# Two transformer layers on one core: setup ordered with the rest, query lengths as scale of the exponential, padded streams

## The chip, the cores and the metric

One NeuronCore of a Trainium2 chip runs the whole program. The time is that of the device, in microseconds; lower is better. The engines have short names: PE is TensorE, ACT ScalarE, DVE VectorE, POOL GpSimd, and SP the queue that issues the DMAs.

## The reference, cut to what matters

The input is 16 sequences of 256 tokens with 128 channels. First a mixing step is computed and added to each sequence, between two modulated layer norms. Then two layers follow, each with windowed attention (8 heads of 64, a query sees its own and the preceding 64 tokens' window) and a gated feed-forward (hidden size 341).

```python
h = shift_token(x)                      # upper 64 channels come from the token before
q, k, v = split(h @ wqkv)               # 3 x 512
q = l2norm(q) * qs;  k = l2norm(k) * ksc
q, k = rotary_xpos(q, k)
o = local_attention(q, k, v)            # softmax over q . k * 8, masked
x = x + o @ wo
h = shift_token(x)
h = (h - mu) / sqrt(var + 1e-5) * lg + lb
a, g = split(h @ w1 + b1)
x = x + (a * gelu(g)) @ w2 + b2
```

The outer part is an adaLN block: shift, scale and gate come from silu(c) @ wmod, per sequence; the output is the input, the gated mixing step and the gated feed-forward part together.

## The kernel before

The work comes in eight half-units of two sequences (512 tokens, four tiles of 128). A "turn" has four slots; slots 0 and 1 do layer 1's projections and layer 0's feed-forward of the two half-units of one unit, slots 2 and 3 layer 0's projections and layer 1's feed-forward, and attention runs one slot behind the projections it needs. So there are 16 attention passes of four tiles, 16 feed-forwards and 16 projection blocks of four tiles, in a pipeline over six lists of steps.

What runs in which order is written out by hand for each engine: `ORDER["pe"]`, `ORDER["act"]`, `ORDER["dve"]` and `ORDER["pool"]` each hold six lists, and `every_turn` issues their steps in that order. The engines meet only through semaphores, so a step waits in its engine's queue for what it needs, and all behind it wait too. SP has no list: it issues loads and stores slot by slot (lines 632 to 661 and `turn`).

Streams are held transposed (channels on partitions, tokens along the free axis), in `y_new` and `y_t`. Matrix products with w_qkv and w1 are taken in three parts: both operands are split into a rounded high part and a low part (`h_hi`, `h_lo`, `wq_hi`, `wq_lo`, `w1_hi`, `w1_lo`).

- *Setup* (lines 699 to 717 on PE, 935 on ACT, 1131 to 1188 on DVE, 1431 to 1448 on POOL) runs ahead of the lists, except two parts of DVE's (`finish_setup`), which follow two steps of the first list. It turns the parameter rows into columns, makes modulation and gates, the guides' unit lengths (by Newton steps on DVE), the rotary tables, and the high and low parts of the weights.
- *Projections*: "split" shifts the stream into `shifted` by two ACT copies (983, 984), DVE rounds it (1380), POOL takes the low part (1483). Per tile and q or k, ACT squares (1083) and for q copies (1087), DVE multiplies by the rotary tables (1391, 1393) and sums the squares per head (1398), POOL multiplies the cosine part of q (1491) and adds (1494) into `qk`. ACT copies v (1093) and the half tile that the next tile's window reads into `v_cross` (1092).
- *Unit lengths*: per pair of tiles DVE bounds the sums (1404), POOL raises 32 columns to the power -0.5 (1454), and DVE multiplies q and k of both tiles by the root (1195).
- *Attention*, per tile: "turn" transposes q and k (PE 696, ACT 950 and 954), "score" puts mask and products into PSUM (746, 759), DVE takes the negated maximum (1215), ACT four exponentials for each of two halves (964), "flip" transposes them (696, 972), "mix" multiplies by v (785), DVE divides (1223, 1227), "out" transposes (978), and "project" after four tiles multiplies by w_o (727); DVE adds it to the stream (1207).
- *Feed-forward*: the shift again (983, 984), transposes, statistics and norm (1235 to 1244), transposes back, an ACT evacuation with gain and bias (997), DVE rounding (1265), POOL's low part (1470), three chunks up with Gelu (795 to 797, 1012, 1273), down (831), sum (1280).

The few lines on which the attention's edit turns:

```python
act.activation(probs[:, ring, hh, :], banks[m][:, hh * P:(hh + 1) * P], ACT.Exp,
               bias=neg_max[:, ring, hh:hh + 1], scale=1.0)
...
return pool.tensor_tensor(to, of, minus_half[:, 0:of.shape[-1]], ALU.pow)
```

## Time and profile before

| | |
|---|---|
| median of three runs | 967.34 us (966.5 to 968.35) |
| the profiled execution | 966.96 us, its span 965.0 us |
| mean granted TensorE clock | 0.942 of full |
| busy: PE, DVE, ACT, POOL | 786.4, 668.0, 659.3, 539.6 us |

Busy time of PE is modelled from pipelined matmuls. An arrow in a row names what ended the idle time before an instruction. The chain is followed back from the last instruction to what released each step; "issue" in it is time for which the profile shows nothing that was waited for. L1207 is line 1207 of the kernel.

### The profile page before, as it was taken

How to read it: one execution, taken by the hardware profiler on the slowest of the kernel's cores; microseconds unless marked ns; L12 is line 12 of the kernel's file. 1: busy time of each engine (PE TensorE's matmuls, PEld its weight loads, DVE VectorE, ACT ScalarE, POOL GpSimd, SP SyncE). 2: the span in 40 equal slices, each digit the busy share in tenths (PEclk: the TensorE clock that was granted, in tenths of full speed). 3: DMA queues.
4: the chain of work that ended last, by engine and by line, in shares of the span. 5: the costliest groups of instructions: out<-in, count | busy, mean ns of one | idle time of the engine just before them, and what ended most of it. 6: DMA issues, size and time to landing. Idle time of an engine off the chain costs nothing.

```text
span 965.0 us, 19306 instructions
## 1 busy us (share of the span) xinstructions
PE 786.4 (81%) x7151; PEld 556.3 (58%) x7151; DVE 668.0 (69%) x1588; ACT 659.3 (68%) x1545; POOL 539.6 (56%) x324
## 2 busy tenths in 40 slices
PE   4456788879889989888969979888888989888874
PEld 4334566656556666655657656656565666656543
DVE  4566876685687877586887967486787776676732
ACT  0234766867576985877786886877675887868672
POOL 2046853493956653394985643293966690576600
PEclk9668789999899999999999999999999999999997
DMA  6000000000000000000000000000000000000000
GB/s 206 0 12 1 12 2 1 1 1 2 1 2 1 23 2 22 2 1 1 1 1 2 23 1 23 1 2 1 1 1 2 12 2 13 2 1 2 1 1 22
DMA packets 12275, 9.85 MB, mean 10 GB/s; under 512 B 1040, under 2 KB 11288, under 8 KB 12184
## 3 DMA queue, kind: packets, MB, share of 16 engines
q1 hardware_dynamic: 12184, 8.64, 3.0%
q8 instruction: 57, 0.93, 0.4%
q14 instruction: 34, 0.28, 0.1%
HBM read 6.54 MB, written 2.10 MB: 9 GB/s over the span
## 4 chain that ended last, share of the span: by engine, by line
PE 40%; DVE 20%; ACT 19%; issue 11%; POOL 9%; DMA 0%; SPq 0%; POOLq 0%; ACTq 0%; DVEq 0%
ACT probs L964 7%; PE pair L696 6%; PE mixed L727 5%; POOL qk L1494 4%; PE dense L831 4%; PE pair L759 3%; DVE space L1393 3%; DVE q_norm L1398 3%; PE dense L795 3%; PE dense L796 2%; PE dense L797 2%; DVE qk L1195 2%; PE dense L908 2%; ACT squares L1083 2%; ACT probs_t L972 2%
## 5 line engine op out<-in xcount | busy, mean ns | idle before, releaser
L1494 POOL TENSOR_TENSOR qk<-space 128x512 f32<-128x512 f32 x128 | 186.4, 1463 | 58.0 <-DVE q_norm L1398 55.1
L1454 POOL TENSOR_TENSOR root<-power,minus_half 128x32 f32<-128x32 f32 x32 | 174.0, 5438 | 4.6 <-DVE power L1404 4.6
L964 ACT ACTIVATE probs<-pair,neg_max 128x128 f32<-128x128 f32 x512 | 138.3, 402 | 18.9 <-DVE neg_max L1215 18.5
L1393 DVE TENSOR_TENSOR space<-dense,tables 128x512 f32<-128x512 f32 x128 | 87.5, 684 | 36.9 <-ACT space L1087 35.2
L908 PE MATMUL dense<-wq_hi,h_hi 128*128 128x512 f32 x192 | 90.2, 470 | 26.6 <-DVE space L1393 10.9
L1491 POOL TENSOR_TENSOR space<-space,tables 128x512 f32<-128x512 f32 x64 | 82.7, 1293 | 50.7 <-ACT space L1087 50.7
L696 PE MATMUL pair<-eye_s,probs 128*128 128x128 f32 x512 | 80.9, 292 | 34.9 <-ACT probs L964 34.7
L1215 DVE TENSOR_REDUCE neg_max<-pair 128x4 f32<-128x512 f32 x128 | 82.0, 684 | 35.2 <-PE pair L759 35.1
L1083 ACT ACTIVATE squares<-dense 128x512 f32<-128x512 f32 x128 | 79.1, 618 | 39.5 <-PE dense L910 38.6
L696 PEld LDWEIGHTS pair<-eye_s,probs 128*128 128x128 f32 x512 | 59.1, 146 | 56.2 <-ACT probs L964 51.9
L1398 DVE TENSOR_REDUCE q_norm<-squares 128x8 f32<-128x512 f32 x128 | 86.4, 675 | 0.0
L1195 DVE TENSOR_TENSOR qk<-qk,root 128x2048 f32<-128x2048 f32 x32 | 81.1, 2534 | 1.7 <-POOL root L1454 1.7
L909 PE MATMUL dense<-wq_lo,h_hi 128*128 128x512 f32 x192 | 78.4, 409 | 0.0
L910 PE MATMUL dense<-wq_hi,h_lo 128*128 128x512 f32 x192 | 78.3, 408 | 0.0
L1483 POOL TENSOR_TENSOR h_lo<-shifted,h_hi 128x512 fp32r<-128x512 f32 x16 | 20.3, 1268 | 103.3 <-DVE h_hi L1380 103.3
L972 ACT ACTIVATE probs_t<-pair 128x512 f32<-128x512 f32 x128 | 72.5, 645 | 4.4 <-PE pair L696 3.6
L1273 DVE SCALAR_TENSOR_TENSOR space<-dense,columns,space 128x512 f32<-128x512 f32 (+1 forms) x48 | 35.9, 749 | 56.3 <-ACT space L1012 45.7
L759 PEld LDWEIGHTS pair<-k_t,q_t 64*64 64x64 f32 x2048 | 55.2, 133 | 27.1 <-issue 27.1
L759 PE MATMUL pair<-k_t,q_t 64*64 64x128 f32 (+1 forms) x2048 | 70.7, 263 | 0.0
L696 PE MATMUL pair<-eye_s,qk 128*128 128x128 f32 x512 | 65.4, 275 | 5.3 <-issue 2.8
L696 PEld LDWEIGHTS pair<-eye_s,qk 128*128 128x128 f32 x512 | 57.1, 141 | 18.6 <-issue 10.7
L727 PE MATMUL mixed<-o_t,wo_s 128*128 128x512 f32 x128 | 62.4, 634 | 5.4 <-ACT o_t L978 5.4
(166 smaller groups left out, 1809.2 us busy)
## 6 DMA issues: line engine op xcount, KB each, us to landing
x_in<-n_L_attn_embeddings_dram SPq DMA_DIRECT2D x8, 256.0 KB, 3.0
out_dram<-hn SPq DMA_DIRECT2D x8, 256.0 KB, 2.4
qk<-in_L_ffn_wqkv_dram SPq DMA_DIRECT2D x1, 1536.0 KB, 6.2
qk<-in_L_ffn_w_dram SPq DMA_DIRECT2D x1, 682.0 KB, 7.5
wo_s<-in_L_ffn_wo_dram SPq DMA_DIRECT2D x2, 256.0 KB
o_t<-in_L_wmod_dram SPq DMA_DIRECT2D x1, 384.0 KB, 3.3
probs<-const_rotary_dram SPq DMA_DIRECT2D x1, 256.0 KB, 3.6
band_s<-const_band_dram SPq DMA_DIRECT2D x1, 256.0 KB, 7.8
```

The source lines that it names most:

```text
L696: last = pe.transpose(to[:, k * P:(k + 1) * P], rows(k), eye_s[:, :])
L727: last = pe.matmul(mixed[:, :], wo_s[:, layer, k, :], o_t[:, k, :], start=(k == 0), stop=(k == 3))
L759: last = pe.matmul(banks[m][w * WIN:(w + 1) * WIN, hh * P:hh * P + n], q_t[rows, t % 2, hh, w * WIN:(w + 1) * WIN], keys, start=False, sto ...
L908: pe.matmul(to[:, :], h_hi[:, rows], wq_hi[:, layer, cols], start=True, stop=False)
L964: last = act.activation(probs[:, ring, hh, :], banks[m][:, hh * P:(hh + 1) * P], ACT.Exp, bias=neg_max[:, ring, hh:hh + 1], scale=1.0)
L972: act.activation(probs_t[:, 2 * (t % 2) + m, :, :], banks[m][:, :].rearrange("p (k n) -> p k n", k=4), ACT.Copy).then_inc(flip_kept, 1)
L1083: last = act.activation(squares[:, m, :], src[:, :], ACT.Square)
L1195: dve.tensor_tensor(rows, rows, root[:, :].rearrange("p (h o) -> p h o", o=1) .broadcast_to([P, 4 * HEADS, DH]), ALU.mult).then_inc(qk_rea ...
L1393: dve.tensor_tensor(turned_s[:, t % 2, m, :].rearrange("p (h a b) -> p h a b", h=HEADS, a=2), halves[:, :, ::-1, :], rot(layer, t, 2 * m + 1),
L1398: dve.tensor_reduce(q_norm[:, 16 * (t % 2) + 8 * m:16 * (t % 2) + 8 * m + 8], squares[:, m, :].rearrange("p (h d) -> p h d", h=HEADS), AX_ ...
L1454: return pool.tensor_tensor(to, of, minus_half[:, 0:of.shape[-1]], ALU.pow)
L1494: pool.tensor_tensor(qk[s][:, t, m * INNER:(m + 1) * INNER], turned_c[:, t % 2, m, :], turned_s[:, t % 2, m, :], ALU.add).then_inc(added, 1)
```

## The change

All four order lists are written anew, with finer steps: turn, flip and mix are each split in two halves (the second number of `3:a.flip.0.1`), feed-forward "up" on PE in gate and value part, and the projections' work on DVE and POOL in "tile", "norm", "cos", "add", "root" and "unit". Gelu's three steps follow each other on ACT with only copies between. Setup becomes steps in the first list, each with its own semaphore: the roundings of w_qkv are on ACT, the guides' root is a power on POOL, and a step "bias" folds the feed-forward norm's gain and bias into w1 and b1.

The streams get a column of zeros in front of each sequence (`SEQ + 1`), and every shift is read in place: the rounding is two DVE copies of 64 partitions each, the low part is half on POOL and half on DVE, and the feed-forward's first transposes are eight matmuls against halves of the identity. `v_cross` is written by DMAs from `v`, on SP's queue, between loads and stores. The inverse root is by a seed (DVE) and three Newton steps (POOL), per stream and pair of tiles; the query's root is the scale of the exponentials, and the maximum is multiplied by it; keys are multiplied tile by tile.

```diff
-        y_new = [sb(f"y_new{s}", [P, 2, SEQ]) for s in range(2)]
-        y_t = [sb(f"y_t{s}", [P, 2, SEQ]) for s in range(2)]
+        y_new = [sb(f"y_new{s}", [P, 2, SEQ + 1]) for s in range(2)]
+        y_t = [sb(f"y_t{s}", [P, 2, SEQ + 1]) for s in range(2)]
...
+            def cross_values(i, slot, p):
+                s = stream(slot)
+                if runs(i, slot, (PROJ,), turns):
+                    for t, half_ in ((2 * p, 1), (2 * p + 1, 0)):
+                        sp.wait_ge(*read_at(i, slot, (PROJ, "tile", t, 2)))
+                        rows = slice(WIN * half_, WIN * half_ + WIN)
+                        sp.dma_start(v_cross[s][rows, p, :, :], v[s][rows, t, :, :]).then_inc(v_crossed[s][p], 16)
+            for i in range(turns + 1):
+                for slot in range(4):
+                    cross_values(i, slot, 0)
+                    if slot > 1:
+                        s = stream(slot)
+                        if runs(i, slot, (STORE,), turns):
+                            store_result(i, slot)
+                        if i < turns - 1:
+                            sp.wait_ge(x_used[s], i + 1)
+                            load_x(i + 1, s)
+                    cross_values(i, slot, 1)
...
-                    pe.wait_ge(qk_ready, 2 * before + t // 2 + 1)
+                    if m == 0:
+                        pe.wait_ge(added, 2 * tau + 1)
+                    else:
+                        pe.wait_ge(keys_ready, tau + 1)
...
-                    done(turn_four(to, lambda k: flat(shifted)[:, k * P:(k + 1) * P]),
-                         i, slot, step)
+                    for k in range(TILES):
+                        at = (k % 2) * P
+                        for part in range(2):
+                            last = pe.matmul(to[:, k * P + part * WIN:k * P + (part + 1) * WIN],
+                                             y_t[stream(slot)][:, k // 2, at + 1 - part:at + 1 - part + P],
+                                             eye_s[:, part * WIN:(part + 1) * WIN], start=True, stop=True)
+                    done(last, i, slot, step)
...
-                                                  bias=neg_max[:, ring, hh:hh + 1], scale=1.0)
+                                              bias=neg_max[:, ring, hh:hh + 1],
+                                              scale=query_root(s, t, m)[:, hh:hh + 1])
...
-                    act.activation(hn[:, :], src[:, :], ACT.Identity, scale=columns[:, ROW_LN_G + layer:ROW_LN_G + layer + 1],
-                                   bias=columns[:, ROW_LN_B + layer:ROW_LN_B + layer + 1]).then_inc(empty(i, slot, step), 1)
+                    wait_split_free(act, i, slot, FF)
+                    act.wait_ge(*filled_at(i, slot, step))
+                    act.activation(h_hi[:, :], bank(i, slot, step)[:, :], ACT.Copy).then_inc(ff_hi, 1)
...
-                        act.activation(v_cross[s][half_rows, t // 2, :, 0:DH], heads[half_rows], ACT.Copy)
...
+                                      ALU.max, negate=True).then_inc(max_self, 1)
+                    dve.wait_ge(max_self, 2 * tau + m + 1)
+                    dve.wait_ge(qk_rooted, 2 * before + t // 2 + 1)
+                    dve.tensor_tensor(neg_max[:, ring, :], neg_max[:, ring, :], query_root(s, t, m),
+                                      ALU.mult).then_inc(maxed, 1)
...
+                elif what == "lo":
+                    dve.wait_ge(ff_hi, before + 1)
+                    src = bank(i, slot, (FF, "norm"))
+                    dve.tensor_tensor(h_lo[:, :], src[:, :], h_hi[:, :].bitcast(F32),
+                                      ALU.subtract).then_inc(empty(i, slot, (FF, "norm")), 1)
...
+                    keys = qk[s][:, t, INNER:].rearrange("p (h d) -> p h d", d=DH)
+                    dve.tensor_tensor(keys, keys, key_root(s, t).rearrange("p (h o) -> p h o", o=1)
+                                      .broadcast_to([P, HEADS, DH]), ALU.mult).then_inc(keys_ready, 1)
...
+            def unit_root(to, pair_):
+                y, z = to[:, 0, :], to[:, 1, :]
+                count = NEWTON * pair_ + 1
+                pool.wait_ge(qk_seeded, pair_ + 1)
+                pool.tensor_tensor(z, y, half[:, :], ALU.mult).then_inc(qk_newton, 1)
+                pool.wait_ge(qk_newton, count)
+                for k in range(3):
+                    pool.tensor_tensor(scratch[:, :], y, z, ALU.mult).then_inc(qk_newton, 1)
+                    pool.wait_ge(qk_newton, count + 1)
+                    pool.tensor_tensor(scratch[:, :], threes[:, :], scratch[:, :], ALU.subtract).then_inc(qk_newton, 1)
+                    pool.wait_ge(qk_newton, count + 2)
+                    if k < 2:
+                        pool.tensor_tensor(to[:, :, :], to[:, :, :], scratch[:, :].rearrange("p (o h) -> p o h", o=1)
+                                           .broadcast_to([P, 2, 32]), ALU.mult).then_inc(qk_newton, 1)
+                        count = count + 3
+                        pool.wait_ge(qk_newton, count)
+                    else:
+                        pool.tensor_tensor(y, y, scratch[:, :], ALU.mult).then_inc(qk_rooted, 1)
...
-                        pool.wait_ge(summed, 2 * tau + m + 1)
+                        if before >= 2:
+                            pool.wait_ge(turned, 8 * (before - 2) + 2 * t + m + 1)
+                        pool.wait_ge(*read_at(i, slot, (PROJ, "tile", t, m)))
```

## Rows read from the trace of the kernel before

**Rows 1.** The page, part 1: busy us, share of the span, instructions, by engine.
```profile
PE 786.4 (81%) x7151; PEld 556.3 (58%) x7151; DVE 668.0 (69%) x1588; ACT 659.3 (68%) x1545; POOL 539.6 (56%) x324
```

**Rows 2.** The page, part 4: the chain that ended last, by engine.
```profile
PE 40%; DVE 20%; ACT 19%; issue 11%; POOL 9%; DMA 0%; SPq 0%; POOLq 0%; ACTq 0%; DVEq 0%
```

**Rows 3.** Windows: busy us (instructions) per engine, granted clock, DMA share, GB/s.
```profile
0.00:61.00 61.00, 25.22 (x95) 20.34 (x95) 31.17 (x113) 9.88 (x27) 11.02 (x26) 0.75 0.28 86
61.00:151.40 90.40, 69.83 (x550) 50.06 (x550) 66.69 (x164) 53.88 (x143) 56.79 (x37) 0.83 0.01 4
151.40:939.10 787.70, 679.15 (x6472) 478.21 (x6471) 561.88 (x1290) 587.61 (x1364) 469.52 (x261) 0.98 0.02 5
939.10:965.00 25.90, 12.19 (x40) 7.69 (x38) 8.27 (x22) 7.97 (x12) 2.27 (x2) 0.74 0.07 20
```

**Rows 4.** Line 1207, the residual sum after attention: durations, first and last start.
```profile
L1207 DVE TENSOR_TENSOR y_t<-y_new,mixed x8: 674/684/689, 151.4 to 848.8; 128x512 f32<-128x512 f32 x8
L1207 DVE TENSOR_TENSOR y_t<-y_t,mixed x8: 671/686/690, 260.0 to 939.1; 128x512 f32<-128x512 f32 x8
```

**Rows 5.** Waits of PE from 150 to 900 us: total, times, longest.
```profile
PE pair L696 <- ACT probs L964: 23.8, 44, 2.3
PE mixed L785 <- ACT probs_t L972: 12.4, 16, 2.1
PE pair L746 <- ACT k_t L954: 11.0, 16, 1.5
```

**Rows 6.** Instruction groups of ACT: count, busy us, mean ns, idle time before.
```profile
L983 ACT ACTIVATE shifted<-y_t 64x512 f32<-64x512 f32 x24 | 15.1, 628 | 28.2 <-DVE y_t L1207 22.7 <-DVE y_t L1280 5.5
...
L1092 ACT ACTIVATE v_cross<-dense 64x512 f32<-64x512 f32 x64 | 38.2, 596 | 8.4 <-PE dense L910 6.2
...
L964 ACT ACTIVATE probs<-pair,neg_max 128x128 f32<-128x128 f32 x512 | 138.3, 402 | 18.9 <-DVE neg_max L1215 18.5
...
L1030 ACT ACTIVATE y_new<-dense,mod 128x256 f32<-128x256 f32 x16 | 8.2, 572 | 20.0 <-PE dense L696 20.0
...
L1108 ACT ACTIVATE hn<-y_t,mod 128x256 f32<-128x256 f32 x16 | 7.3, 508 | 7.2 <-DVE y_t L1280 7.2
```

**Rows 7.** Instruction groups of DVE.
```profile
L1195 DVE TENSOR_TENSOR qk<-qk,root 128x2048 f32<-128x2048 f32 x32 | 81.1, 2534 | 1.7 <-POOL root L1454 1.7
...
L1380 DVE CAST h_hi<-shifted 128x512 fp32r<-128x512 f32 x16 | 7.7, 483 | 8.0 <-ACT shifted L984 8.0
```

**Rows 8.** Small DVE products: line 1315's group, then line 1317's min, median, max.
```profile
L1315 DVE TENSOR_TENSOR col<-col,root_n 128x4 f32<-128x4 f32 x8 | 3.2, 402 | 1.4 <-POOL root_n L1454 1.4
...
L1317 DVE TENSOR_TENSOR col<-col x8: 161/163/1143, 33.9 to 708.8; 128x4 f32<-128x4 f32 x8
```

**Rows 9.** Instruction groups of POOL.
```profile
L1494 POOL TENSOR_TENSOR qk<-space 128x512 f32<-128x512 f32 x128 | 186.4, 1463 | 58.0 <-DVE q_norm L1398 55.1
...
L1454 POOL TENSOR_TENSOR root<-power,minus_half 128x32 f32<-128x32 f32 x32 | 174.0, 5438 | 4.6 <-DVE power L1404 4.6
...
L1470 POOL TENSOR_TENSOR h_lo<-hn,h_hi 128x512 fp32r<-128x512 f32 x16 | 23.7, 1484 | 61.0 <-DVE h_hi L1265 61.0
...
L1444 POOL TENSOR_TENSOR tables<-probs 128x128 f32<-128x128 f32 x8 | 3.3, 450 | 0.0
```

**Rows 10.** The chain in order of time: start us, us, what.
```profile
190.91 5.29 issue
...
771.77 5.23 issue
```

**Rows 11.** The page, part 6, DMA issues: KB each, us to landing.
```profile
x_in<-n_L_attn_embeddings_dram SPq DMA_DIRECT2D x8, 256.0 KB, 3.0
```

**Rows 12.** Timeline, start and tail: start us, us, engine, line, idle before.
```profile
28.89 3.36 DVE L1182 TENSOR_TENSOR wq_lo<-qk,wq_hi 128x3072 fp32r<-128x3072 f32 x1
...
939.84 0.63 ACT L983 ACTIVATE shifted<-y_t 64x512 f32<-64x512 f32 x1 [2.46 <-DVE y_t L1207]
...
949.82 0.79 PE L795 MATMUL dense<-h_hi,w_hi 128*128 128x512 f32 x1 [2.74 <-POOL h_lo L1470]
```

More of the change, by code:

```diff
@@ new lines @@
+        2:a.mix.3.1 3:a.turn.0.0 2:proj.tile.1.2 2:proj.tile.2.0 2:a.out.3 2:proj.tile.2.1 2:a.project
+        2:proj.tile.2.2 2:proj.tile.3.0 2:proj.tile.3.1 2:proj.tile.3.2 3:a.turn.0.1 3:a.turn.1.0
+        3:a.turn.1.1 2:ff.norm 3:a.score.0 2:new.mix 3:a.score.1 2:new.sum 2:ff.up.0.0 2:ff.up.0.1
+        2:ff.up.1.0 2:ff.up.1.1 2:ff.up.2.0 2:ff.up.2.1 2:ff.down 2:new.stream 3:a.flip.0.0 3:a.flip.0.1
+        2:store.turn 3:ff.stats 3:a.mix.0.0 3:a.mix.0.1 3:a.flip.1.0 3:proj.tile.0.0 3:a.flip.1.1
@@ new lines @@
+        2:proj.tile.1.1 2:a.mix.2.0 2:a.mix.2.1 2:a.flip.3.0 2:a.flip.3.1 2:a.out.2 2:a.mix.3.0 2:a.mix.3.1
+        3:a.turn.0.0 2:proj.tile.1.2 2:a.out.3 2:proj.tile.2.0 2:a.project 2:proj.tile.2.1 2:proj.tile.2.2
+        2:proj.tile.3.0 2:proj.tile.3.1 2:proj.tile.3.2 3:a.turn.0.1 3:a.turn.1.0 2:ff.norm 3:a.turn.1.1
+        3:a.score.0 2:new.mix 3:a.score.1 2:new.sum 2:ff.up.0.0 2:ff.up.0.1 2:ff.up.1.0 2:ff.up.1.1
+        2:ff.up.2.0 2:ff.up.2.1 2:ff.down 2:new.stream 3:a.flip.0.0 3:a.flip.0.1 2:store.turn 3:ff.stats
@@ L145 @@
+        2:a.flip.2.0 2:a.flip.2.1 2:a.mix.2.0 2:a.flip.3.0 2:a.mix.2.1 2:a.flip.3.1 2:a.out.2 2:a.mix.3.0
+        2:a.mix.3.1 2:store.turn 2:a.out.3 2:a.project 3:ff.stats 3:ff.norm 3:ff.up.0.0 3:ff.up.0.1
+        3:ff.up.1.0 3:ff.up.1.1 3:ff.up.2.0 3:ff.up.2.1 3:ff.down 3:store.turn"""),
     ],
@@ L281 @@
-        2:new.stream 2:ff.up.0 2:ff.up.1 2:ff.up.2 3:a.unit 2:ff.down 3:proj.split 3:a.score.0 3:a.score.1
-        2:store.turn 2:proj.keep 3:proj.tile.0.0 3:proj.tile.0.1 3:a.mix.0 3:proj.tile.1.0 3:new.stats
-        3:proj.tile.1.1 3:new.turn 3:proj.rsqrt.0 3:proj.tile.2.0 3:proj.tile.2.1 3:a.mix.1 3:ff.stats
-        3:a.score.2 3:ff.norm 3:a.score.3 3:proj.unit.0 3:new.dots 3:a.mix.2 3:proj.tile.3.0 3:new.sims
-        3:a.mix.3 3:new.weights 3:ff.hi 3:proj.tile.3.1 3:new.gate 3:new.again 3:ff.up.0 3:proj.rsqrt.1
@@ L297 @@
-        2:new.weights 2:proj.tile.0.1 2:proj.tile.1.0 2:proj.tile.1.1 2:proj.rsqrt.0 2:proj.tile.2.0
-        2:proj.tile.2.1 2:ff.stats 2:a.score.2 2:a.score.3 2:proj.unit.0 2:ff.norm 2:a.mix.2 2:proj.tile.3.0
-        2:a.mix.3 2:proj.tile.3.1 2:new.gate 2:ff.hi 2:new.again 2:a.project 2:proj.rsqrt.1 2:new.stream
-        2:ff.up.0 2:ff.up.1 2:ff.up.2 3:a.unit 2:ff.down 3:proj.split 3:a.score.0 3:a.score.1 2:store.turn
-        2:proj.keep 3:proj.tile.0.0 3:proj.tile.0.1 3:a.mix.0 3:proj.tile.1.0 3:proj.tile.1.1 3:proj.rsqrt.0
@@ new lines @@
+        2:proj.tile.3.0 2:proj.tile.3.1 2:proj.norm.3.0 2:proj.norm.3.1 2:proj.root.1 2:ff.lo 3:a.score.0.0
+        2:new.gate 2:proj.unit.2 2:proj.unit.3 2:ff.up.0 2:ff.up.1 2:new.again 2:ff.up.2 3:a.score.0.1
+        2:new.stream 2:ff.down 3:a.score.1.0 3:a.score.1.1 2:store.turn 3:proj.hi 2:proj.keep 3:proj.lo
+        3:ff.stats 3:a.mix.0.0 3:a.mix.0.1 3:ff.norm 3:a.mix.1.0 3:proj.tile.0.0 3:a.mix.1.1 3:proj.norm.0.0
+        3:proj.norm.0.1 3:proj.tile.0.1 3:new.stats 3:a.score.2.0 3:a.score.2.1 3:proj.norm.1.0
@@ new lines @@
+        2:proj.tile.3.0 2:proj.tile.3.1 2:proj.norm.3.0 2:proj.norm.3.1 2:proj.root.1 2:ff.lo 3:a.score.0.0
+        3:a.score.0.1 2:new.gate 2:proj.unit.2 2:proj.unit.3 2:ff.up.0 2:ff.up.1 2:new.again 2:ff.up.2
+        3:a.score.1.0 2:new.stream 2:ff.down 3:a.score.1.1 2:store.turn 3:proj.hi 2:proj.keep 3:proj.lo
+        3:ff.stats 3:a.mix.0.0 3:a.mix.0.1 3:ff.norm 3:a.mix.1.0 3:proj.tile.0.0 3:a.mix.1.1 3:proj.norm.0.0
+        3:proj.norm.0.1 3:proj.tile.0.1 3:new.stats 3:a.score.2.0 3:a.score.2.1 3:proj.norm.1.0
@@ new lines @@
+        2:proj.tile.3.0 2:proj.tile.3.1 2:proj.norm.3.0 2:proj.norm.3.1 2:proj.root.1 2:ff.lo 3:a.score.0.0
+        2:new.gate 2:proj.unit.2 2:proj.unit.3 2:ff.up.0 2:ff.up.1 2:new.again 2:ff.up.2 3:a.score.0.1
+        2:new.stream 2:ff.down 3:a.score.1.0 3:a.score.1.1 2:store.turn 3:proj.hi 2:proj.keep 3:proj.lo
+        3:ff.stats 3:a.mix.0.0 3:a.mix.0.1 3:ff.norm 3:a.mix.1.0 3:proj.tile.0.0 3:a.mix.1.1 3:proj.norm.0.0
+        3:proj.norm.0.1 3:proj.tile.0.1 3:a.score.2.0 3:a.score.2.1 3:a.mix.2.0 3:proj.norm.1.0
@@ L789, in attention @@
+                    last.then_inc(mixed_full, 1)
                 elif what == "out":
```

1323 lines of the change are left out of this document (768 added, 555 removed).

## The prediction

> **What bounds the kernel now.** I read the engines' shares first. TensorE (PE) is busy 786.4 of 965.0 us [rows 1], far more than any other, so the question is why it is idle for 179 us. The chain that ended last is not mainly TensorE's: PE 40%, DVE 20%, ACT 19%, POOL 9%, issue 11% [rows 2]. Set against the busy times, 183 of ACT's 659 us (0.28), 193 of DVE's 668 (0.29) and 87 of POOL's 540 (0.16) stand on it. So this is a ring of short hand-overs with TensorE in most of them, not one saturated engine. The windows say where TensorE idles: 35.8 us before the first projection, 20.6 until the first residual sum, 108.5 in the 788 us between the first and last residual sum, 13.7 in the tail [rows 3]. The middle holds 15 intervals between the 16 attention passes' sums (151.4 to 939.1 us, 52.5 each) [rows 4]. The waits there name ACT first: 23.8 us for the exponentials, 12.4 for the turned probabilities, 11.0 for the turned keys [rows 5]. The granted clock is 0.75, 0.83, 0.98 and 0.74 in the four windows [rows 3]: low where TensorE waits a lot, near full in the middle.
>
> **The change part by part.** The sum is made against the profiled execution, 966.96 us around a span of 965.0; the median of the three runs is 0.38 us higher, which I neglect. I convert busy time that leaves or joins an engine into path time by the shares above, since I can't know which copies of an operation stay exposed under new orders. That is the weakest step.
>
> **ACT, removed.** The shift of the stream by one token took two activations per half-unit, 32 times: 0.63 us each [rows 6], 40 us; the padded streams are read in place. The 64 copies into v_cross, 38.2 us [rows 6], become DMAs. The layer norm's gain and bias fold into w1 and b1, which makes its evacuation plain: some 3 us. Together -81.
>
> **ACT, added.** Each of the 512 exponentials gets a second pointer operand. What that costs no row shows for Exp. The nearest pair is one pointer against two over 256 columns: 508 and 572 ns, busy 7.3 and 8.2 us for 16, so 0.06 each [rows 6]. Below, nothing if the overlap of the back-to-back exponentials (402 ns long, 270 ns apart in busy time [rows 6]) hides it; above, 0.13, that whole overlap. I take 0.06, as the pair differs in just this: +31 us. Net ACT -50, times 0.28: **-14**.
>
> The Trainium skill, "ScalarE: Activation LUTs", section "What ACT_TABLE_LOAD costs", prices each pointer operand at about 93 ns and the overlap at about 93. By it ACT would gain 48 us and the net be 5 us worse on the path; the one-pointer exponential of 402 ns fits its 280 + 0.833 per column (387) within 15 ns, the pair's 64 ns does not reach 93.
>
> **DVE, removed.** The unit multiply covered q and k of two tiles in 2534 ns, 32 times, 81.1 us [rows 7]. Now only keys, per tile: a quarter, 0.63, plus a start of about 0.1, 64 times, 47 us. So -34.
>
> **DVE, added.** 128 small products of the negated maximum with the root. The nearest are products of two SBUF inputs on four columns: one line's took 402 ns in the mean, the other's 161 to 1143 with a median of 163 [rows 8]. So most are short and a few wait for something, which I suspect to be POOL at work on the same memory. Bounds 0.16 and 1.14; I take the mean, 0.40: +51. The projections' rounding becomes two half-height copies instead of one of 483 ns [rows 7], +8, and its upper half of the low part comes to DVE, +11; the feed-forward's low part comes from POOL and its rounding leaves, +4; the root's seed adds a second small operation 32 times, +6. Net +46, times 0.29: **+13**. DVE ends near 714 us, the second busiest.
>
> **POOL.** The power operation took 5438 ns, 32 times, 174.0 us [rows 9]. In its place come ten dependent small products (eight of 32 columns, two of 64). 128 columns took 450 and 512 columns 1463 at worst-mixed mean [rows 9], about 2.6 ns a column over a start of 0.12, so 0.2 and 0.29 us, 2.2 us in all, and some 0.07 for each of nine waits: 2.8. Bounds: 2.0, and 4.5 if each costs what 128 columns do. So -84. The feed-forward's low part leaves, -23.7 [rows 9]; the lower-half one still has 512 columns and stays. On the chain the power also hides in pieces called issue: five of 3.9 to 5.3 us, 25 us, the first at 190.91 and the last at 771.77, each just behind a rotary add [rows 10]. With them the power's share is 0.22, so 84 times 0.22 plus 24 times 0.16: **-22**. The add no longer waits for the norms (55.1 us of POOL's idle time [rows 9]); as DVE does the same work before it in another order, I cost that at nothing.
>
> **TensorE.** The shift moves into eight narrow matmuls instead of four transposes per feed-forward, at most +7 us of busy time, partly in its idle time: **+3**. Turn, flip and mix are split into halves that the new order interleaves with projections. The three waits they aim at sum to 47 us in the middle [rows 5]; I give a third: **-16**, between +10 (a worse order) and -35.
>
> **The v_cross DMAs** (64 of 133 KB) wait on SP behind a tile's read, and the second pair of each half-unit behind a store and a load. The mix that needs them is a pass later. A load of 256 KB landed in 3.0 us [rows 11] against a pass of 52.5: nothing. If that cover fails, each exposed one costs 3 to 5 us, at most one a pass.
>
> **Start.** DVE's 3.36 us of weight work at 28.89 us stood ahead of the first new unit's norms [rows 12]; roundings move to ACT, and the first transposes go ahead of the gate broadcast. But new steps are queued too: ACT's two roundings wait for all weights ahead of the first turn, POOL's tables come ahead of the first root, and DVE scales w1 between the similarities and the weights. I take **-5**, between +4 and -12. **Tail.** From the last sum to the first up product: the shift's two activations (the first at 939.84) go, 1.25 us, and h_hi and h_lo come straight out of PSUM, some 1.3 less before the first product at 949.82 [rows 12]: **-2.6**.
>
> Sum: -14 + 13 - 22 + 3 - 16 - 5 - 2.6 = -43.6, so 923 us. About 0.2% (2 us) is what a measurement of this kernel can tell from no change.
>
> **Rivals.**
> *TensorE is fed.* If the relief of ACT and POOL opens the ring, middle idle time falls from 108.5 to about 45, the stretch before by 10, start and tail as above: 966.96 - 63 - 10 - 7.6 = 886. For it: 47 us of waits on three ACT steps, and ACT's net loss. Against: DVE becomes longer.
> *Handed on to DVE.* The product stands between maximum and exponential, the key multiply between add and turn; if DVE's share on the chain rises to half for the added 80 us (+40 for +23) and the new order gives nothing, the sum is -14 + 30 - 22 + 3 - 7.6 = -10.6: 956.
> *Slower: each softmax half is on the ring.* The place is maximum, product, four exponentials, before every flip. Its price is 0.40 + 4 x 0.13 = 0.92 us, 128 times, 118 us if all are exposed. The remaining relief is ACT -81 x 0.28, DVE's unit -34 x 0.29, POOL -22, start and tail -7.6: -62. It decides from 68 exposed halves of 128; with 90, +83 - 62 = +21: 988. Against it, TensorE waited only 44 times for exponentials in the middle [rows 5]; DVE at 79% of a shorter span, for it.
> By the skill's 93 ns the price would be 0.77 and the turning point 81 halves; that lowers this rival a little.
> *It doesn't do what it says.* If the Newton steps take the 5 us that the power took (ten at 0.45 and waits), POOL's 84 is gone: 923 + 18 = 941, inside the forecast's range.
>
> **How the numbers follow.** The forecast with its bounds, 900 to 945: 0.47. Fed, 872 to 900: 0.18. Handed on, 945 to 965: 0.18. No measurable change: 0.04. Slower, above 969: 0.13. Faster is 0.83 in all. The range 872 to 968 leaves out most of the slower case and the far end of the fed one, some 0.17. The likeliest time is 923 us.
>
> **What would show it.** The pass interval between residual sums goes from 52.5 to about 50. ACT's busy time is near 609 us, DVE's near 714, POOL's near 432, TensorE's near 790. The exponentials are 0.45 to 0.5 us long; a spacing of 0.35 or more would show the second operand exposed. The small product is near 0.4 us in the mean with long ones beside POOL's work. The ten root steps take under 3 us from first to last. TensorE's waits for probs and probs_t fall; its waits for DVE rise. If mixes wait on a DMA, the cover of v_cross was wrong. Middle idle time above 100 us would show that relief of ACT and POOL was not what the ring wanted; under 60, that my conversion by shares was too timid.

## The result, and the profile after

The changed kernel is **slower**: 991.75 us in the median (988.47 to 993.45) against 966.92 of the kernel before, timed beside it, a ratio of 1.0251 (95% interval 1.0221 to 1.0281). 923 us was forecast. The profiled execution has a span of 989.3 us, 24.3 more than before (965.0).

First the shares of the page of the changed kernel, engines and then the chain that ended last, by engine and by line.

```profile
PE 813.3 (82%) x7323; PEld 583.4 (59%) x7367; DVE 729.0 (74%) x1803; ACT 629.5 (64%) x1413; POOL 421.3 (43%) x600
...
PE 42%; DVE 20%; ACT 18%; issue 16%; POOL 3%; SPq 0%; DMA 0%; DVEq 0%; ACTq 0%; POOLq 0%
ACT probs L1190 9%; PE pair L878 7%; PE mixed L892 4%; PE pair L932 4%; PE dense L1092 3%; DVE space L1650 2%; DVE q_norm L1659 2%; DVE neg_max L1448 2%; DVE qk L1680 2%; PE dense L1094 2%; PE dense L1093 2%; ACT probs_t L1199 2%; PE pair L957 2%; PE dense L967 2%; PE dense L878 2%
```

The busy times moved nearly as forecast: ACT fell to 629.5 (609 forecast), POOL to 421.3 (432), DVE rose to 729.0 (714), only TensorE rose by 27 instead of 4 [rows 1]. What did not follow is the time. POOL's share of the chain went from 9% to 3% and ACT's stayed [rows 2], and the largest entry of a line is the exponentials. The 16% of "issue" hold one piece of 33.65 us, from 935.44 us on, through which the chain could not be followed; the shares are to be read with that gap.

The windows, cut at the same events as in [rows 3] (first projection, first and last residual sum):

```profile
0.00:61.00 61.00, 27.52 (x124) 22.44 (x125) 31.61 (x106) 12.57 (x30) 13.86 (x31) 0.75 0.26 82
61.00:124.40 63.40, 49.05 (x437) 34.74 (x437) 47.51 (x125) 38.48 (x94) 31.20 (x42) 0.92 0.07 16
124.40:964.70 840.30, 723.73 (x6718) 517.36 (x6758) 642.00 (x1552) 571.90 (x1280) 375.19 (x528) 0.98 0.06 15
964.70:989.30 24.60, 13.00 (x48) 8.85 (x48) 7.93 (x21) 6.53 (x10) 1.01 (x1) 0.72 0.04 11
```

The first residual sum comes 27 us earlier, but the 15 intervals behind it take 56.0 us each, not 52.5. Part of that is work that the new orders moved behind the first sum: by the second sum the gain is 7 us (192.7 against 199.6). The loss is in the steady passes. TensorE's idle time in the middle is 840.3 - 723.7 = 116.6 us, above the 100 at which the prediction would call the relief of ACT and POOL not what the ring wanted. As a share of the stretch it is 14%, as before (108.5 of 787.7). The tail is 1.3 us shorter (2.6 forecast).

The groups that answer to [rows 6] to [rows 9], with two that are new (statistics in narrow pieces, product on the maximum):

```profile
L1190 ACT ACTIVATE probs<-pair,neg_max,root 128x128 f32<-128x128 f32 x512 | 190.3, 494 | 28.3 <-DVE neg_max L1452 28.2
...
L1452 DVE TENSOR_TENSOR neg_max<-neg_max,root 128x4 f32<-128x4 f32 x128 | 30.2, 236 | 4.4
...
L1680 DVE TENSOR_TENSOR qk<-qk,root 128x512 f32<-128x512 f32 x64 | 72.8, 1169 | 1.7 <-POOL root L1761 1.5
...
L1800 POOL TENSOR_TENSOR qk<-space 128x512 f32<-128x512 f32 x128 | 170.9, 1349 | 61.8 <-DVE space L1650 59.3
...
L982 PE MATMUL dense<-eye_s,y_t 128*128 128x64 f32 x256 | 33.0, 285 | 4.2 <-DVE weighed L1576 3.4 <-DVE y_t L1440 0.8
L982 PEld LDWEIGHTS dense<-eye_s,y_t 128*128 128x128 f32 x256 | 31.5, 201 | 6.3 <-issue 4.7 <-DVE y_t L1440 1.6
```

An exponential takes 494 ns instead of 402, and 190.3 / 512 = 0.37 us of busy time instead of 0.27: the second operand is exposed in full, 0.10 us each where 0.06 were taken. The product is short (0.24, not 0.40). The key product is long (1.17, not 0.73). TensorE's waits for the exponentials between 150 and 900 us, which were to fall, rose from 23.8 [rows 5] to 33.5 us; those for the turned probabilities fell from 12.4 to 3.3. The pieces of the statistics leave 256 matmul records, sixteen per feed-forward: each of the eight plain f32 matmuls shows twice, with a weight load each time, where a transpose shows once (512 records for the 512 of the probabilities).

One stretch of the timeline shows the ring at work (start us, us, engine, line; idle time before and its releaser):

```profile
430.07 0.68 DVE L1448 TENSOR_REDUCE neg_max<-pair 128x4 f32<-128x512 f32 x1
430.78 0.18 DVE L1452 TENSOR_TENSOR neg_max<-neg_max,root 128x4 f32<-128x4 f32 x1
...
431.00 2.90 ACT L1190 ACTIVATE probs<-pair,neg_max,root 128x128 f32<-128x128 f32 x8 [2.79 <-DVE neg_max L1452]
...
432.56 0.66 PE L878 MATMUL pair<-eye_s,probs 128*128 128x128 f32 x4
432.97 3.01 POOL L1800 TENSOR_TENSOR qk<-space 128x512 f32<-128x512 f32 x2
433.19 1.06 DVE L1452 TENSOR_TENSOR neg_max<-neg_max,root 128x4 f32<-128x4 f32 x1
433.95 0.42 PEld L878 LDWEIGHTS pair<-eye_s,probs 128*128 128x128 f32 x4 [0.98 <-ACT probs L1190]
```

Maximum, product, eight exponentials (two halves) in 2.90 us, transposes; ACT had waited 2.79 us for the product and TensorE waits again before the second half. The product at 433.19 takes 1.06 us instead of 0.16 to 0.18 while POOL's add runs beside it.

### The profile page after: what moved, and what is told of

The parts are those of the page before. It is cut to its first block, busy times and chain, and to the rows that moved or that the text cites. A ratio compares the mean times of both kernels' runs of the same rounds, so it can differ in the third digit from the quotient of the medians.

```text
span 989.3 us, 20633 instructions
## 1 busy us (share of the span) xinstructions
PE 813.3 (82%) x7323; PEld 583.4 (59%) x7367; DVE 729.0 (74%) x1803; ACT 629.5 (64%) x1413; POOL 421.3 (43%) x600
## 4 chain that ended last, share of the span: by engine, by line
PE 42%; DVE 20%; ACT 18%; issue 16%; POOL 3%; SPq 0%; DMA 0%; DVEq 0%; ACTq 0%; POOLq 0%
ACT probs L1190 9%; PE pair L878 7%; PE mixed L892 4%; PE pair L932 4%; PE dense L1092 3%; DVE space L1650 2%; DVE q_norm L1659 2%; DVE neg_max L1448 2%; DVE qk L1680 2%; PE dense L1094 2%; PE dense L1093 2%; ACT probs_t L1199 2%; PE pair L957 2%; PE dense L967 2%; PE dense L878 2%
## 5 line engine op out<-in xcount | busy, mean ns | idle before, releaser
L1190 ACT ACTIVATE probs<-pair,neg_max,root 128x128 f32<-128x128 f32 x512 | 190.3, 494 | 28.3 <-DVE neg_max L1452 28.2
L1800 POOL TENSOR_TENSOR qk<-space 128x512 f32<-128x512 f32 x128 | 170.9, 1349 | 61.8 <-DVE space L1650 59.3
L1092 PE MATMUL dense<-wq_hi,h_hi 128*128 128x512 f32 x192 | 95.9, 499 | 32.7 <-DVE space L1650 27.1
L1741 POOL TENSOR_TENSOR root_n<-power_n,minus_half 128x4 f32<-128x4 f32 x24 | 24.6, 1025 | 184.9 <-DVE power_n L1477 157.9
L1650 DVE TENSOR_TENSOR space<-dense,tables 128x512 f32<-128x512 f32 x128 | 86.9, 680 | 18.3 <-ACT space L1297 18.3
L1199 ACT ACTIVATE probs_t<-pair 128x512 f32<-128x512 f32 x128 | 81.9, 651 | 9.2 <-PE pair L878 9.0
L878 PE MATMUL pair<-eye_s,qk 128*128 128x128 f32 x512 | 77.1, 287 | 12.7 <-ACT o_t L1205 6.8
L1227 ACT ACTIVATE space<-dense,columns 128x512 f32<-128x512 f32 (+1 forms) x48 | 33.0, 686 | 66.4 <-PE dense L969 66.2
L1680 DVE TENSOR_TENSOR qk<-qk,root 128x512 f32<-128x512 f32 x64 | 72.8, 1169 | 1.7 <-POOL root L1761 1.5
L1092 PEld LDWEIGHTS dense<-wq_hi,h_hi 128*128 128x128 f32 x192 | 38.2, 199 | 54.6 <-DVE space L1650 37.3
L1304 ACT ACTIVATE v<-dense 128x512 f32<-128x512 f32 x64 | 39.4, 616 | 32.9 <-PE dense L1094 30.5
```

The lines of the kernel that those rows point to most:

```text
L878: last = pe.transpose(to[:, k * P:(k + 1) * P], rows(k), eye_s[:, :])
L1092: pe.matmul(to[:, :], h_hi[:, rows], wq_hi[:, layer, cols], start=True, stop=False)
L1190: last = act.activation(probs[:, ring, hh, :], banks[m][:, hh * P:(hh + 1) * P], ACT.Exp, bias=neg_max[:, ring, hh:hh + 1], scale=query_ro ...
L1199: act.activation(probs_t[:, 2 * (t % 2) + m, :, :], banks[m][:, :].rearrange("p (k n) -> p k n", k=4), ACT.Copy).then_inc(flip_kept, 1)
L1650: dve.tensor_tensor(turned_s[:, t % 2, m, :].rearrange("p (h a b) -> p h a b", h=HEADS, a=2), halves[:, :, ::-1, :], rot(layer, t, 2 * m + 1),
L1680: dve.tensor_tensor(keys, keys, key_root(s, t).rearrange("p (h o) -> p h o", o=1) .broadcast_to([P, HEADS, DH]), ALU.mult).then_inc(keys_r ...
```

## The experiments

Three theories fit the result: TensorE's own work grew (busy time +26.9, span +24.3, idle time the same); each softmax half is on the ring (the slower rival); the new orders are worse. Every run was timed beside the kernel before, which took 965.5 to 966.9 us; the ratio behind a time is to it. A difference of two kernels timed side by side is of their medians; any other is of their ratios, times 966.

### Parts taken out of the changed kernel

**The pointer and the product.** The first run takes both out, the second the product alone.

```diff
-    ...ALU.max, negate=True).then_inc(max_self, 1)
-dve.wait_ge(max_self, 2 * tau + m + 1)
 dve.wait_ge(qk_rooted, 2 * before + t // 2 + 1)
-dve.tensor_tensor(neg_max[:, ring, :], neg_max[:, ring, :], query_root(s, t, m), ALU.mult).then_inc(maxed, 1)
+    ...ALU.max, negate=True).then_inc(maxed, 1)
...
-    scale=query_root(s, t, m)[:, hh:hh + 1])
+    scale=1.0)                     # first run; second run: scale=ones_s[:, hh:hh + 1]
```

> The changed kernel with the exponentials' scale the constant 1.0 and without the product of the negated maximum with the query roots (the query lengths are left out of the computation). Theory 'TensorE got longer' (its busy time grew by 26.9 us, the span by 24.3, its idle time stayed at 176): nothing of TensorE's own work is removed, so the span stays near 989 us, 980 at the least. Theory 'each softmax half is on the ring' (48 halves wait for the exponentials, 33.5 us between 150 and 900 us): each of 128 halves gets shorter by 4 x 0.10 us of exponentials and by 0.24 us of product with the wait between, some 0.75 us; with 70 of them exposed the span falls by 50 us, to about 940. Theory 'the new orders': 980 to 985.

> The changed kernel without the product on the negated maximum, the exponentials' scale still a pointer, to a column of ones (the query lengths are left out of the computation). It parts the two costs of the last run: by the ring theory about half of that run's gain, 20 to 30 us, is gone with the product (0.24 us and the wait ahead of it, per half), the rest with the pointer (4 x 0.10 us per half). By 'TensorE got longer' and by 'the new orders' it stays within 5 us of 989.

Measured: 961.06 us (ratio 0.9934, 0.9908 to 0.996) and 981.52 (1.0148, 1.0129 to 1.0167). The product is worth about 10 us in the changed kernel, the pointer 20.5, together 30.6. That is more than the whole loss of 24.8, if less than the 50 us expected, and the product's part of it is smaller than expected. The pointer adds 46.5 us to the busy time of the 512 exponentials (143.6 us in the first run, 190.1 in the second); 0.44 of that is seen in the time. Theory "TensorE got longer" falls as the main cause: TensorE's matmuls were left alone. Its waits for the exponentials, over the whole span, show it, first in the changed kernel, then without both:

```profile
PE pair L878 <- ACT probs L1190: 44.0, 65, 3.4
```

```profile
PE pair L878 <- ACT probs L1190: 16.9, 45, 2.6
```

**The narrow pieces.**

```diff
-for k in range(TILES):
-    at = (k % 2) * P
-    for part in range(2):
-        last = pe.matmul(...64 columns..., eye_s[:, part * WIN:(part + 1) * WIN], start=True, stop=True)
-done(last, i, slot, step)
+done(turn_four(to, lambda k: rows_of[:, k // 2, (k % 2) * P + 1:(k % 2) * P + 1 + P]), i, slot, step)
```

> The changed kernel with the feed-forward's statistics turned by four 128-wide transposes of the unshifted stream in the place of sixteen narrow pieces (the token shift is left out there). TensorE's busy time falls by some 22 us (33.0 to about 11), its weight loads by about 24. Theory 'TensorE got longer': the span follows, to about 970. Theory 'ring' or 'orders': the feed-forward is off the ring most of the time, and the span falls by under 6 us, 983 to 989.

Measured: 982.22 us (1.0163, 1.0128 to 1.0197). TensorE's busy time fell by 22.9 us to 790.4, the time by 8.5: less than half. Its wait for the exponentials rose from 44.0 to 55.8 us. TensorE reaches the ring earlier and waits there.

```profile
PE pair L878 <- ACT probs L1185: 55.8, 78, 3.4
```

**Newton's steps.**

```diff
-dve.tensor_scalar(half[:, :], q_norm[:, :], 1e-24, 0.5, ALU.max, ALU.mult).then_inc(seed_self, 1)
-dve.wait_ge(seed_self, pair_ + 1)
-dve.tensor_scalar(root[s][p][:, 0, :].bitcast(I32), half[:, :].bitcast(I32), -0.5, RSQRT_SEED, ...)
+dve.tensor_scalar(half[:, :], q_norm[:, :], 1e-24, None, ALU.max).then_inc(seed_self, 1)
...
+inverse_root(to[:, 0, :], half[:, :]).then_inc(qk_rooted, 1)     # POOL, for the ten products
```

> The changed kernel with GpSimd's power in the place of the seeds and Newton's steps, nothing left out. My prediction priced the root at 5.44 us against 2.8 and gave Newton 22 us of the path: the span would be near 1010 us. If the chain over each root is hidden by the spread orders, it stays within 5 us of 989. If the many small operations of GpSimd disturb VectorE (the key product took 1169 ns a piece where 730 was expected, the seeds 531), the key product gets shorter and the span falls by 5 to 15 us.

Measured: 1037.08 us (1.0729, 1.0707 to 1.0751), 46 us more. No expectation held. The key product did not get shorter either (1325 ns), so Newton's small operations are not what stretches it. DVE now stands before it:

```profile
DVE qk L1677 <- POOL root L1738: 44.2, 24, 3.5
```

**All three parts together:** the edits of the first and the third run of this section at once.

```diff
-dve.tensor_tensor(neg_max..., query_root(s, t, m), ALU.mult)
-    scale=query_root(s, t, m)[:, hh:hh + 1])
+    scale=1.0)
+done(turn_four(to, ...), i, slot, step)     # for the eight narrow matmuls
```

> The changed kernel with three parts out together: the product, the pointer and the narrow pieces of the statistics (query lengths and the token shift of the feed-forward are left out). Alone they were worth 10.2, 20.5 and 9.5 us. If they add up, the span falls by 40 us, to 951. If TensorE's work is what is left once the ring is shorter, the pieces are worth their whole 22 us now, and it comes to 940. If the order alone binds by then, 955 to 961.

Measured: 957.88 us (0.9909, 0.989 to 0.9928), 33 us less. With the ring short, the pieces are worth only 2.4 us more, which can't be told from nothing: the interval with the pieces in is 0.9908 to 0.996. TensorE's work does not bind here either.

### Parts put into the kernel before

**Newton alone.** All 32 roots, in two alternating tiles.

```diff
-dve.tensor_scalar(power[:, :], q_norm[:, :], 1e-24, None, ALU.max).then_inc(qk_powered, 1)
+dve.tensor_scalar(power[:, :], q_norm[:, :], 1e-24, 0.5, ALU.max, ALU.mult).then_inc(seed_self, 1)
+dve.wait_ge(seed_self, pair_ + 1)
+dve.tensor_scalar(root_y[pair_ % 2][:, 0, :].bitcast(I32), power..., -0.5, RSQRT_SEED, ...).then_inc(qk_powered, 1)
...
-inverse_root(root[:, :], power[:, :]).then_inc(qk_rooted, 1)
+pool.tensor_tensor(z, y, power[:, :], ALU.mult)     # and nine more, as in the change
```

> The kernel before with one part of the change: seeds on VectorE and Newton's steps on GpSimd in the place of the power, over the whole 32 roots, nothing else changed. In the changed kernel the power instead of Newton cost 45 us (1037 against 991.8). If a root lies on the path in the order of before too, as the prediction had it (22 us on the way from 5.44 us to 2.8 us per root), the span falls by 20 to 25 us, to about 945; if Newton is worth in before what it is in after, to about 922. If it was only the new orders that exposed the root, 960 to 967.

Measured: 965.24 us (0.9985, 0.9968 to 1.0001): not to be told from no change. POOL's share of the chain fell from 9% to 2%, and the five issue pieces of [rows 10] are gone from it (the longest left ahead of the tail is 2.1 us). The chain by engine:

```profile
PE 41%; DVE 22%; ACT 21%; issue 11%; POOL 2%; DMA 0%; SPq 0%; POOLq 0%; ACTq 0%; DVEq 0%
```

So another chain, just as long to within 1.3 us, stood beside it, with more of ACT and DVE.

**The pointer alone.**

```diff
-    ACT.Exp, bias=neg_max[:, ring, hh:hh + 1], scale=1.0)
+    ACT.Exp, bias=neg_max[:, ring, hh:hh + 1], scale=ones_s[:, hh:hh + 1])
```

> The kernel before with the exponentials' scale a pointer to a column of ones, nothing else changed. In the changed kernel the pointer cost 20.5 us (981.5 against 961.1) where the prediction gave the net of ScalarE's gains and losses 0.28 of its busy time: 0.28 x 512 x 0.09 = 13 us. If the softmax ring is as exposed in before, 985 to 988; by the chain share 980; if the new orders alone put the exponentials on the path, 967 to 972.

Measured: 1001.88 us (1.0364, 1.0348 to 1.038), +35 us, more than the highest expectation. The group, and TensorE's wait:

```profile
L965 ACT ACTIVATE probs<-pair,neg_max,ones_s 128x128 f32<-128x128 f32 x512 | 184.5, 485 | 17.4 <-DVE neg_max L1218 17.1
```

```profile
PE pair L697 <- ACT probs L965: 65.6, 84, 5.1
```

The same wait in the kernel before, over its whole span:

```profile
PE pair L696 <- ACT probs L964: 34.7, 54, 4.7
```

The chain with the pointer:

```profile
PE 41%; ACT 30%; DVE 16%; issue 10%; POOL 1%; DMA 0%; SPq 0%; ACTq 0%; POOLq 0%; DVEq 0%
ACT probs L965 15%; PE pair L697 7%; PE mixed L728 5%; PE dense L832 3%; PE pair L760 2%; PE dense L909 2%; PE dense L796 2%; ACT probs_t L974 2%; ACT squares L1085 2%; PE dense L797 2%; PE dense L798 2%; DVE qk L1198 2%; DVE space L1396 2%; ACT space L1089 2%; PE mixed L786 2%
```

46.2 us of busy time (138.3 [rows 6] to 184.5) became 35 us of time, 0.76 of it. The exponentials' line took 15% of the chain; in the kernel before it had 7%:

```profile
ACT probs L964 7%; PE pair L696 6%; PE mixed L727 5%; POOL qk L1494 4%; PE dense L831 4%; PE pair L759 3%; DVE space L1393 3%; DVE q_norm L1398 3%; PE dense L795 3%; PE dense L796 2%; PE dense L797 2%; DVE qk L1195 2%; PE dense L908 2%; ACT squares L1083 2%; ACT probs_t L972 2%
```

**The transfers for v_cross:**

```diff
-act.activation(v_cross[s][half_rows, t // 2, :, 0:DH], heads[half_rows], ACT.Copy)
...
+sp.wait_ge(*read_at(i, slot, (PROJ, "tile", t, 2)))
+sp.dma_start(v_cross[s][rows, p, :, :], v[s][rows, t, :, :]).then_inc(v_crossed[s][p], 16)
...
+if m == 0 and t % 2:
+    pe.wait_ge(v_crossed[s][t // 2], 32 * (before // 2 + 1))
```

> The kernel before with the crossed values copied by 64 transfers on SyncE's queue in the place of ScalarE's copies of half the rows (38 us of ScalarE), nothing else changed. By the prediction's conversion (0.28 of busy time) the span falls by some 11 us, to 956. If ScalarE's copies were hidden, it stays within 3 us of 967; if a mix has to wait for the transfer, it is longer, 970 to 990.

Measured: 962.03 us (0.9956, 0.9941 to 0.9971), -4.5. ACT lost 32.3 us of busy time (659.3 to 627.0): 0.14 of it came out as time. No mix waited for a transfer.

**No shifted copies.**

```diff
-shift(y_t[stream(slot)], ff_shifted)
...
-shift((y_t if slot < 2 else y_new)[s], qkv_shifted)
...
-dve.tensor_copy(h_hi[:, :], flat(shifted)).then_inc(qkv_hi, 1)
+dve.tensor_copy(h_hi[:, :], flat((y_t if slot < 2 else y_new)[s])).then_inc(qkv_hi, 1)
```

> The kernel before without ScalarE's shifted copies: the feed-forward's transposes and the projections' split read the stream itself, as one piece (the token shift is left out of the computation). It takes 40 us off ScalarE, as the change does, at no cost elsewhere. By the prediction's conversion (0.28 of busy time) the span falls by 11 us, to 956. If such copies lie beside other work, as ScalarE's crossed copies mostly did (38 us gave 4.5), 962 to 966. If the shift is on the chain from one residual sum to the next projection (32 shifts of 1.3 us), up to 30 us, 937.

Measured: 958.89 us (0.9926, 0.9906 to 0.9947), -6.6, for 39.6 us of ACT's busy time: 0.17.

**The product alone**, by ones, with its wait:

```diff
-    ...ALU.max, negate=True).then_inc(maxed, 1)
+    ...ALU.max, negate=True).then_inc(max_self, 1)
+dve.wait_ge(max_self, 2 * tau + m + 1)
+dve.tensor_tensor(most, most, ones_s[:, :], ALU.mult).then_inc(maxed, 1)
```

> The kernel before with the negated maximum multiplied by a column of ones on VectorE, behind a wait of its own, nothing else changed: the change's product alone. In the changed kernel it was worth 10.2 us (991.8 against 981.5). If that is its price on the ring of either order, 975 to 979. If it is in before what the pointer was there against there (35 against 20.5), some 984. If VectorE's 30 us are beside the ring, 966 to 969.

Measured: 982.14 us (1.0158, 1.0126 to 1.0191), +16. The product took 320 ns in the mean here, 41.0 us of DVE's time.

### Operations against orders

**The change's operations in the orders of before:** the parts above at once (Newton, transfers, pointer, product, no shifted copies, narrow pieces), only the keys multiplied, rounding in two halves of rows, the stream's low part half on POOL and half on DVE. The feed-forward's norm stays as it was; the token shift and the query lengths are left out.

```diff
-rows = qk[s][:, 2 * p:2 * p + 2, :]...              # one product of 2048 elements
+for t in (2 * p, 2 * p + 1):
+    rows = qk[s][:, t, INNER:]...                   # two of 512
...
+for rows in (slice(0, WIN), slice(WIN, P)):
+    last = dve.tensor_copy(h_hi[rows, :], stream_y[rows, :])
```

> The kernel before, in its own orders, with the change's operations: seeds and Newton, transfers for the crossed values, pointer scale and product (both with ones), only the keys multiplied, tile by tile, the stream rounded in two halves of rows and its rest by VectorE and GpSimd half each, no shifted copies, statistics in narrow pieces (the query lengths and the token shift are left out; the feed-forward's norm stays as it was). What the changed kernel has beyond this is the orders, the split steps and the setup. By the sum of the single runs: 967 + 35 (pointer) + 10 (product) + 9 (pieces) - 1 (Newton) - 4.5 (transfers) - 5 to 11 (shift) = 1005 to 1011; then the new orders are worth 13 to 19 us, about the 16 + 5 predicted for orders and setup. If the new orders are worse, it is under 985. If they are worth as much as Newton's 45 us in them suggests, 1030.

Measured: 1011.23 us (1.048, 1.0455 to 1.0505), as the sum of the single runs has it. TensorE's longest wait:

```profile
PE pair L714 <- ACT probs L989: 60.0, 71, 5.3
```

The changed kernel is at 1.0251, so what it has beyond this run is together worth 0.023 of 966, 22 us: its orders, split steps and setup, and the feed-forward's norm (rounding by ACT, low part by DVE), which no run parts from them. "New orders" below means all of this.

**The same with the power**, which undoes the edit shown under Newton:

> The run with the change's operations in the orders of before (1011), with the power in the place of seeds and Newton's steps, nothing else changed. Newton was worth 45 us in the changed kernel, 1.3 in before, 8.7 in before with the transfers (962.0 against 953.4). If the new orders expose the root, it is worth little here: 1012 to 1020. If the change's operations do (the ring longer, the keys multiplied tile by tile), it is worth 40 to 50: 1050 to 1060.

Measured: 1009.14 us (1.043, 1.0394 to 1.0465). The intervals of the two runs touch, and the power is if anything the faster one: Newton is worth nothing here. So it is the **new orders** that expose the root. In them DVE comes to the key product a few short steps behind the seed; in the old ones this wait was 2.7 us in all:

```profile
L1207 DVE TENSOR_TENSOR qk<-qk,root 128x512 f32<-128x512 f32 x64 | 57.5, 939 | 2.7 <-POOL root L1482 2.7
```

With the power the new orders cost 1.0729 - 1.043, 29 us; with Newton they give 22.

### Could the query lengths have stayed with VectorE?

```diff
-keys = qk[s][:, t, INNER:]...                      # 512 elements
+rows = qk[s][:, t, :]...                           # 1024 elements, no product, scale=1.0
...
+ORDER["pe"], ORDER["act"] = queries_later(ORDER["pe"]), queries_later(ORDER["act"])
```

`queries_later` moves each `a.turn.t.0` to just ahead of `a.turn.t.1`. A second run has this move alone.

> The changed kernel with one part undone: queries and keys are both multiplied on VectorE, tile by tile, the exponentials' scale is the constant 1.0 and there is no product; a query's transposes come just ahead of the key's, since they now wait for the root too. Nothing is left out. Without product and pointer the kernel took 961; VectorE gets back 64 multiplications of 512 elements, some 1.15 us each here, 73 us of busy time. At the chain's share of VectorE (0.20) that is 15 us: 976. If VectorE's work lies beside the ring, 962 to 968; if it holds up the maxima as in the rival 'handed on to VectorE', over 990.

> The changed kernel with each query's transposes and their copy moved behind, just ahead of the key's, nothing else changed. The run with both multiplied on VectorE (1012) differs from the one without product and pointer (961) by this move and by VectorE's work on the queries. If the loss came from the work, the move alone costs under 8 us here: 992 to 1000. If it came from the lost overlap, 1020 to 1040.

Measured: 1012.13 us (1.0469, 1.0441 to 1.0498) and 997.45 (1.0306, 1.0264 to 1.0347). The move costs some 5 us. Against the run without product and pointer (0.9934) undoing this part costs 0.0535 of 966, 52 us, of which about 46 are beyond the move: the multiplications of 1024 elements took 1766 ns each, 111.0 us in all, 35 more than that run's 75.9. So under these orders the query lengths cannot go back as they stood (+21 us against the change). Which step behind VectorE's work turns 35 us into 46 was not settled.

### A version that beats both

The edits shown under Newton and under the transfers, both in the kernel before, in its own orders.

> The kernel before with the two parts of the change that made it no slower, Newton's steps and the transfers for the crossed values. Alone they gave 1.3 and 4.5 us. In the run with the transfers alone GpSimd's share of the chain grew from 9 to 12 %, so the power may be what is left there: if the parts help each other, 950 to 957; if they only add up, 960 to 962.

Measured: **953.35 us** (0.9875, 0.9845 to 0.9904), 12 us under the kernel before, with nothing left out of the computation; the two parts alone gave 1.3 and 4.5. With the transfers in, Newton is worth some 8 us (give or take 3): as I read the chains, because ACT's part of the competing one is shorter. The engines and the chain of this version:

```profile
PE 778.6 (82%) x7151; PEld 550.2 (58%) x7151; DVE 681.8 (72%) x1621; ACT 627.6 (66%) x1481; POOL 446.9 (47%) x612
...
PE 41%; DVE 28%; ACT 15%; issue 12%; POOL 2%; DMA 0%; SPq 0%; POOLq 0%; DVEq 0%; ACTq 0%
```

ACT's share went from 19% to 15% and POOL's from 9% to 2%; DVE is the next to look at, with 28%. It takes two parts of the change and neither its orders nor its softmax.

## Why the prediction was wrong

**The step that failed** is the conversion: "I convert busy time that leaves or joins an engine into path time by the shares above", with 0.28 for all of ACT. The prediction called it the weakest step, yet gave it no bounds of its own in the range. Inside ACT the runs show 0.76 for the exponentials in the kernel before (0.44 in the changed one), 0.17 for the shifted copies and 0.14 for v_cross. The change takes away the hidden kind and adds the exposed kind, so the term had the wrong sign.

- **ACT:** forecast -14. Measured singly in the kernel before: copies -4.5, shifts -6.6, pointer +35, together +24. The pointer was forecast at 31 x 0.28 = 9 us. Its true size of 46.2 would have made that 13, so 4 us of the mistake are size (0.09 each, inside the bound of 0.13) and 22 are conversion. The Trainium skill, "ScalarE: Activation LUTs", section "What ACT_TABLE_LOAD costs", has each pointer operand at about 93 ns, which the prediction set aside in favour of its row; with 402 to 494 ns the trace agrees with it, and the pair over 256 columns misled.
- **DVE:** forecast +13, from +46 us of busy time; +61 came. The product was to be 51 us and is 30.2; alone it is +16 of the time in before and +10 in the change, where 51 x 0.29 = 15 was forecast. The key product was mis-sized: 72.8 us instead of 47. So was the seed: its two small operations took 531 and 532 ns in the mean, 34 us in all, against 10.6 for the one before (+23, forecast +6). What the root's seed and the halves cost by themselves was not tried; in the sum of the operations little is left for them (next point but two).
- **POOL:** forecast -22. The ten operations are 2.67 us of busy time per root (85.5 us for 32) and 3.36 us from first to last, where 2.2 and 2.8 were forecast and "under 3" was the sign. That is small against what is missing: POOL lost 118.3 us of busy time with 108 forecast, but in the orders of before the exchange is worth 1.3 us, and that not clear of nothing. The "issue" pieces that were added to the power's share did leave the chain; another chain replaced them. A share of one chain is an upper bound of a gain, not the gain.
- **TensorE:** forecast +3. The pieces cost 8.5, with 22.9 us of busy time where at most 7 were forecast: each matmul shows as two records with a weight load each.
- **Operations in all:** the two kept parts -12.2, shifts -6.6, pointer +35, product +16, pieces +8.5 make +41; measured together +46. Forecast: -20.
- **Orders, start and tail:** forecast -16 - 5 - 2.6 = -23.6; measured -22. Right as a sum, and that is luck. By place, against the run with the change's operations in the orders of before (second residual sum at 203.6, last at 983.6, span 1009.4 us): 11 us up to the second sum (192.7), 8 in the 14 intervals behind it, 1.2 in the tail (20 us between these two executions), where 5, 16 and 2.6 were forecast. And it holds only with Newton's steps. The forecast added the two parts, though one is the condition of the other.
- **v_cross transfers:** cost nothing, as forecast: landing 2.2 us, and no mix waits for one.
- **The rivals.** "Each softmax half is on the ring" had the right place, at 988 us and a chance of 0.13. That its number came so close is luck. Its price per half was 0.92 us; the rows give 4 x 0.10 + 0.24 = 0.64. In the changed kernel pointer and product cost 30.6 us, which is 48 halves at that price and not 90, and the rest of the change gave 6 us and not 62: two errors cancel. What spoke against it, that TensorE waited only 44 times for exponentials [rows 5], was a poor test: with the pointer in before the waits over the span rise from 54 times and 34.7 us to 84 times and 65.6 us. A half that is just in time does not wait, and is exposed to whatever is added. "It doesn't do what it says" fell. "Handed on to DVE" has a part: the product and the long key product are real, but DVE's share of the chain stayed at 20%. (The 79% for DVE in the slower rival's favour does not come out of its rows: 714 of 923 us is 77%.)

## What to carry to other kernels

Price a line, not an engine: before adding anything to an instruction that stands between two hand-overs, ask what share of that line's own busy time lies on the chain, and expect more than that, since the neighbours that were just in time become late (about 0.5 by the chain's 7% of 965 us over 138.3, 0.76 measured there; 0.44 in the changed kernel, so the figure belongs to the orders as well). A relief counts the other way: take its share of one chain as the most that it can give, and look for the chain that takes over. And where a change brings faster steps and tighter orders, they are one item: here the faster root without the orders gave 1 us, and the orders without it cost 29.

## What the hardware showed

- Products of VectorE whose inputs both lie in SBUF get much longer beside GpSimd's work. The key product over 512 elements, minimum, median and maximum:

```profile
L1680 DVE TENSOR_TENSOR qk<-qk,root x64: 677/1110/1814, 74.8 to 933.9; 128x512 f32<-128x512 f32 x64
```

  and the product of four elements, 161 to 1191 ns with a median of 163. In the timeline both are long where POOL's add runs beside them:

```profile
423.36 2.97 POOL L1800 TENSOR_TENSOR qk<-space 128x512 f32<-128x512 f32 x2
423.50 3.37 DVE L1680 TENSOR_TENSOR qk<-qk,root 128x512 f32<-128x512 f32 x2
```

  One long instruction over 2048 elements suffered less (2534 ns, 1.24 ns an element [rows 7]) than the short ones right behind the adds (1169 ns, 2.3 ns an element). Of the 64 key products the 16 during which GpSimd runs nothing take 678 to 693 ns, and all 34 over 780 ns overlap its work for 0.89 us or more. The rotary product L1650 of the same 512 columns, which reads one input from PSUM, overlaps GpSimd's work in 100 of 128 cases and never takes over 693 ns. The seed's first operation, with one input of 32 columns, goes from 164 to 933 ns. That GpSimd's work is the cause is read from these overlaps, not tried by itself.
- A second pointer operand on a ScalarE activation over 128 columns costs 83 to 92 ns of its length and the same 0.09 to 0.10 us of spacing; the overlap of back-to-back activations does not hide it.
- A plain f32 matmul of 64 columns against the identity leaves two records of 285 ns and two weight loads of 201 ns. Four transposes of 128 columns for eight of these took 22.9 us off TensorE's busy time over 16 feed-forwards.
